# Reciprocal roots of a four-layer kernel: from Newton steps on VectorE to a power instruction on GpSimd

## The reference, cut to what matters

```python
# layer 0: attention, then a second norm whose result is added
ln = (h - mu) / jnp.sqrt(var + EPS) * ln_g + ln_b            # before attention
h1 = out + hidden;  h2 = _sln(h1, ...);  return h2 + h1      # after it, over all tokens
# layer 1: attention with q and k normalised over each head's 64 numbers, then 8 experts
(x - m) * jax.lax.rsqrt(v + EPS) * g + b                     # tokens, heads of q and k, experts
# layer 2: attention and feed-forward, each behind a norm
(x - mu) * jax.lax.rsqrt(var + EPS)
# layer 3: the same with a root mean square in place of the variance
x * jax.lax.rsqrt(jnp.mean(x * x, axis=-1, keepdims=True) + EPS)
```

## Time and profile before

| | us |
|---|---|
| median of 3 runs | 3143.8 |
| lowest, highest | 3141.02, 3148.51 |
| the profiled execution's own time | 3146.93 |
| its span, from first to last instruction | 3145.1 |
| TensorE busy | 2813.3 |
| VectorE busy | 1723.7 |
| ScalarE busy | 916.6 |
| GpSimd busy | 332.6 |

### The profile page before, as it was taken

How to read it: one execution, slowest core, us unless ns; L and a number is a source line. 1 busy time by engine, 2 the same in 40 slices (tenths; PEclk the granted TensorE clock), 3 DMA queues, 4 the chain that set the end, 5 groups by cost and what they waited for, 6 DMA issues and landing times.

```text
span 3145.1 us, 68238 instructions
## 1 busy us (share of the span) xinstructions
PE 2813.3 (89%) x27492; PEld 2032.2 (65%) x27492; DVE 1723.7 (55%) x4229; ACT 916.6 (29%) x1647; POOL 332.6 (11%) x390
## 2 busy tenths in 40 slices
PE   7999699999999933998699999998997989979999
PEld 6788556666666631665588888885443877755555
DVE  5666677777777676231444444443333888842221
ACT  2333255555555500221122222222211233311110
POOL 1111001010010101232011111110000111100000
PEclk9999799999999955999799999998998899989999
DMA  5000000000000031342300000000000000000000
GB/s 184 0 0 0 8 17 27 24 23 27 20 27 20 18 114 50 85 126 47 109 0 0 0 0 0 0 0 1 0 0 0 1 0 0 0 1 14 14 14 14
DMA packets 62313, 77.40 MB, mean 25 GB/s; under 512 B 12640, under 2 KB 52064, under 8 KB 61728
## 3 DMA queue, kind: packets, MB, share of 16 engines
q1 hardware_dynamic: 56096, 67.88, 6.5%
q0 software_dynamic: 6144, 8.52, 1.4%
HBM read 59.33 MB, written 17.06 MB: 24 GB/s over the span
## 4 chain that ended last, share of the span: by engine, by line
PE 54%; DVE 29%; issue 9%; ACT 4%; DVEq 2%; DMA 1%; POOL 0%; SPq 0%; ACTq 0%; POOLq 0%
PE psS L1079 7%; PE psW L293 6%; PE psW L286 5%; DVE work L653 5%; PE psP L463 4%; PE psP L1052 4%; PE psP L1046 4%; PE psS L1073 4%; PE psO L1046 4%; PE psO L1052 3%; DVE work L655 2%; PE psO L408 2%; PE psP L455 2%; PE psO L326 2%; PE psP L392 2%
## 5 line engine op out<-in xcount | busy, mean ns | idle before, releaser
L293 PE MATMUL psW<-r,work 128*128 128x512 f32 (+1 forms) x1280 | 557.0, 567 | 5.5 <-DVE work L690 3.7
L286 PE MATMUL psW<-work,r 128*128 128x128 f32 x3072 | 388.2, 285 | 21.7 <-DVE work L642 16.1
L286 PEld LDWEIGHTS psW<-work,r 128*128 128x128 f32 x3072 | 366.2, 198 | 42.4 <-DVE work L642 31.0
L931 ACT ACTIVATE work<-work 128x512 f32<-128x512 f32 x256 | 161.2, 630 | 628.4 <-DVE work L655 628.4
L293 PEld LDWEIGHTS psW<-r,work 128*128 128x128 f32 x1280 | 225.4, 192 | 173.3 <-issue 156.9
L979 POOL TENSOR_TENSOR work<-work 128x512 f32<-128x512 f32 x128 | 130.7, 1042 | 1274.1 <-DVE work L664 1274.1
L1079 PE MATMUL psS<-r,work 128*128 128x256 f32 x1024 | 225.3, 381 | 6.1 <-DVE work L1149 5.3
L1079 PEld LDWEIGHTS psS<-r,work 128*128 128x128 f32 x1024 | 193.2, 190 | 36.0 <-DVE work L1149 6.1
L392 PE MATMUL psP<-consts,work 128*128 128x128 f32 x1024 | 153.1, 285 | 55.7 <-ACT work L931 50.0
L655 DVE TENSOR_TENSOR work<-psS,work 128x512 f32<-128x512 f32 x256 | 177.0, 692 | 16.3
L653 DVE TENSOR_REDUCE work<-psS 128x8 f32<-128x512 f32 x256 | 174.8, 683 | 11.5 <-PE psS L372 9.7
(11 more groups left out here) (194 smaller groups left out, 4236.9 us busy)
## 6 DMA issues: line engine op xcount, KB each, us to landing
r<-in_l_fc SPq DMA_DIRECT2D x16, 1024.0 KB
work<-mod_rows SPq DMA_DIRECT2D x64, 128.0 KB, 2.9
r<-in_l_w SPq DMA_DIRECT2D x2, 3072.0 KB, 14.6
x<-in_x SPq DMA_DIRECT2D x8, 512.0 KB, 10.0
gather_table<-work SPq DMA_DIRECT2D x32, 128.0 KB, 1.8
moe_sum<-work SPq DMA_DIRECT2D x32, 128.0 KB, 1.7
x<-moe_sum SPq DMA_DIRECT2D x4, 1024.0 KB, 9.4
out<-x SPq DMA_DIRECT2D x8, 512.0 KB, 2.9
```

The costliest lines, as they stand in the source:

```text
L286: ins = nc.tensor.matmul(ps[:, q * P:(q + 1) * P], w[:, k, lo + q * P:lo + (q + 1) * P], L.hT[:, k, :], start=(k == 0), stop=(k == KC - 1))
L293: ins = nc.tensor.matmul(ps[:, 0:width], L.hT[:, k, :], w[:, k, lo:lo + width], start=(k == 0), stop=(k == KC - 1))
L931: nc.scalar.activation(E, E, ACT.Exp, scale=scale).then_inc(L.s[f"exp{i}"].sem, 1)
```

## The change

All 50 roots move to GpSimd. `dve_rsqrt` and its buffer go. A root is now two instructions on GpSimd: an addition of eps, and, after a wait for that addition's semaphore, a power with exponent -0.5. Both take their constant from a column of a small array, broadcast to the shape, which GpSimd fills with three memsets at its start.

For ten of the roots VectorE raises a semaphore (`dve_ask_root`) and waits for another (`dve_take_root`). In layer 0's loop the request is made at the end of steps 4, 12 and 20 and the wait stands at the end of steps 5, 13 and 21; in between GpSimd does the root, behind its bias sum of step 4, 12 and 20, and its program of layer 0 is written out tile by tile instead of run as a loop. In all other places VectorE waits at once.

In layer 1, GpSimd waits for the fourth sum (semaphore r3) and for the variance (new semaphore var), behind the two multiplications of the step. The division by 64 goes: the variance is multiplied by 64 when it is copied, eps is 64 times as large, the root of the variance is multiplied by 8 when it is copied back, and the gains of q and k get a factor 8 in the setup. In the experts, GpSimd's step t first does the root of expert t+1, then the gathers of expert t+2 and the scatters of expert t.

```diff
-        def dve_rsqrt(ch, out, var):
...
+        def dve_ask_root(v, name):
+
+            v.sem_inc(ro["var"], 1)
+
+        def dve_take_root(v, name):
+            v.wait_ge(ro["root"], 2 * (ROOTS.index(name) + 1))
+
+        def root_on_pool(g, out, var, eps, done, count):
+
+            def const(name):
+                at = ROOT_CONSTS.index(name)
+                one = root_consts[:, at:at + 1]
+                return (one.unsqueeze(2) if len(var.shape) == 3 else one).broadcast_to(list(var.shape))
+
+            nc.gpsimd.tensor_tensor(out, var, const(eps), ALU.add).then_inc(done.sem, 1)
+            after(g, done, 2 * count - 1)
+            nc.gpsimd.tensor_tensor(out, out, const("minus_half"), ALU.pow).then_inc(done.sem, 1)
+
+        def pool_root(g, name, out, var):
+            g.wait_ge(ro["var"], ROOTS.index(name) + 1)
+            root_on_pool(g, out, var, "eps", Signal(ro["root"], 0), ROOTS.index(name) + 1)
...
-                    nc.vector.tensor_copy(L.ss33[:, 32:33], mv[:, 0, 1:2])
-            after(v, L.s["r3"], n + 1)
-            ch.link(nc.vector.tensor_scalar(L.ss, L.ss, 1.0 / 64, None, ALU.mult))
-            dve_rsqrt(ch, L.ss33, L.ss33)
+                    nc.vector.tensor_scalar(L.ss33[:, 32:33], mv[:, 0, 1:2], 64.0, None, ALU.mult
+                                            ).then_inc(L.s["var"].sem, 1)
+            after(v, L.s["root"], (n + 1) * 2)
             if norm_too:
-                nc.vector.tensor_copy(rstd[:, bass.ds(n + 2, 1)], L.ss33[:, 32:33])
+                nc.vector.tensor_scalar(rstd[:, bass.ds(n + 2, 1)], L.ss33[:, 32:33], 8.0, None, ALU.mult)
...
+            def head_roots(n, norm_too):
+
+                after(g, L.s["r3"], n + 1)
+                if norm_too:
+                    after(g, L.s["var"], n + 1)
+                root_on_pool(g, L.ss33, L.ss33, "eps64", L.s["root"], n + 1)
...
+                    if L.li == 1 and ahead:
+                        head_roots(t + 1, ahead == 3)
                     return
...
+                if L.li == 0 and t % 8 == 4 and t < NT - 8:
+                    k = t // 8 + 1
+                    pool_root(g, f"l0 {k}", rstd[:, 8 * k:8 * k + 8], moments[:, 8 * k:8 * k + 8, 1])
...
-                    ch.link(ins)
-                    dve_rsqrt(ch, Q.stat[:, :, 2], Q.stat[:, :, 1])
+                    ins.then_inc(Q.s["f_var"].sem, 1)
+                    after(v, Q.s["f_root"], (n + 1) * 2)
...
+            def root(n, u):
+
+                after(g, Q.s["f_var"], n + 1)
+                root_on_pool(g, Q.stat[:, :, 2], Q.stat[:, :, 1], "eps", Q.s["f_root"], n + 1)
+
             def first():
                 gather(0, 0, 0)
                 gather(1, 1, 0)
+                root(0, 0)
 
             def step(t, u, half, ahead):
+                if ahead:
+                    root(t + 1, 1 - u)
                 if ahead == 2:
                     gather(t + 2, u, half + 1)
```

More of the change, by code:

```diff
@@ L221, in build_program @@
         st = sems("st", "out tab gates idx rows")
+        ro = sems("ro", "consts var root")
+        ROOT_CONSTS = ["minus_half", "eps", "eps64"]
+        root_consts = sb("root_consts", [P, 3])
         chain_dve = sem("chain_dve")
@@ L268, in __init__ @@
                     self.s |= signals("rows_in", NT * 32)
+                    self.s |= signals("root", NT * 2)
                 self.loads = {0: 2, 1: 3, 2: 4, 3: 5}[li]
@@ L551, in four @@
             return ap.rearrange("p k (b n) -> p k b n", n=N)
-        def dve_rsqrt(ch, out, var):
[L556 to L573, removed]
+        ROOTS = ["l0 0", "l0 1", "l0 2", "l0 3", "l1 all", "l1 two", "l2", "l2ff", "l3", "l3ff"]
+        def dve_ask_root(v, name):
[13 more added lines that the diff above has]
+            root_on_pool(g, out, var, "eps", Signal(ro["root"], 0), ROOTS.index(name) + 1)
         def dve_moments(ch, t):
@@ L603, in dve_first_block @@
                 dve_group_moments(ch, i)
-            dve_rsqrt(ch, rstd[:, 0:8], moments[:, 0:8, 1])
+            dve_ask_root(v, "l0 0")
+            dve_take_root(v, "l0 0")
         def dve_next_block(v, ch, t):
             k = t // 8 + 1
-            if k == 4 or t % 8 not in (1, 3, 5):
+            if k == 4 or t % 8 not in (1, 3, 4, 5):
+                return
+            if t % 8 == 4:
+                dve_ask_root(v, f"l0 {k}")
                 return
             if t % 8 == 5:
-                dve_rsqrt(ch, rstd[:, 8 * k:8 * k + 8], moments[:, 8 * k:8 * k + 8, 1])
+                dve_take_root(v, f"l0 {k}")
                 return
@@ L779, in first @@
                 if L.li == 1:
-                    dve_rsqrt(ch, L.rstd0, moments[:, :, 1])
+                    dve_ask_root(v, "l1 all")
+                    dve_take_root(v, "l1 all")
                     for n in range(2):
                         dve_second_norm(v, ch, L, n)
-                    dve_rsqrt(ch, rstd[:, 0:2], moments[:, 0:2, 1])
+                    dve_ask_root(v, "l1 two")
+                    dve_take_root(v, "l1 two")
                 elif L.li != 0:
-                    dve_rstd(ch, rms=L.li == 3)
+                    dve_rstd(v, ch, f"l{L.li}", rms=L.li == 3)
                 dve_norm(v, ch, L, 0)
@@ L967, in masks @@
                 ins.then_inc(L.s["mask"].sem, 1)
-            def first():
+            def head_roots(n, norm_too):
[3 more added lines that the diff above has]
+                root_on_pool(g, L.ss33, L.ss33, "eps64", L.s["root"], n + 1)
+            def first():
+                if L.li == 1:
+                    pool_root(g, "l1 all", L.rstd0, moments[:, :, 1])
+                    pool_root(g, "l1 two", rstd[:, 0:2], moments[:, 0:2, 1])
+                    head_roots(0, True)
+                if L.li == 2:
+                    pool_root(g, "l2", rstd[:, :], moments[:, :, 1])
+                if L.li == 3:
+                    pool_root(g, "l3", rstd[:, :], rstd[:, :])
                 if not L.wide:
@@ L986, in step @@
                                         ALU.add).then_inc(L.s["xb"].sem, 1)
+                if L.li == 0 and t % 8 == 4 and t < NT - 8:
+                    k = t // 8 + 1
+                    pool_root(g, f"l0 {k}", rstd[:, 8 * k:8 * k + 8], moments[:, 8 * k:8 * k + 8, 1])
+            if L.li == 0:
+                first()
+                for t in range(NT):
+                    step(t, min(3, NT - 1 - t), t > 0)
+                return
             tiles(g, NT, first, step)
@@ L1020, in __init__ @@
                     self.s |= signals("f_sc", NG * 64)
+                    self.s |= signals("f_var", NG)
+                    self.s |= signals("f_root", 2 * NG)
                     self.s |= signals("f_in0 f_in1 f_ga0 f_ga1", NG // 2 * 64)
@@ L1735, in _ @@
             g.wait_ge(ld["small"], 48)
+            for i, value in enumerate((-0.5, EPS, 64 * EPS)):
+                nc.gpsimd.memset(root_consts[:, i:i + 1], value).then_inc(ro["consts"], 1)
+            g.wait_ge(ro["consts"], 3)
+            pool_root(g, "l0 0", rstd[:, 0:8], moments[:, 0:8, 1])
             g.wait_ge(ld["rows"], 32)
@@ L1744, in _ @@
             pool_attention(g, L[2])
+            pool_root(g, "l2ff", rstd[:, :], moments[:, :, 1])
             following(g, "l2ff")
             pool_attention(g, L[3])
+            pool_root(g, "l3ff", rstd[:, :], rstd[:, :])
 def host_arrays(I):
```

11 lines of the change are left out of this document (6 added, 5 removed), and 2 rows, old and new, of the table W.

## The result

The changed kernel takes 3264.9 us in the median of four runs (3262.9 to 3267.7), against 3146.2 us (3141.0 to 3149.5) for the kernel before on the same chip. The ratio is 1.038, with a 95% interval from 1.036 to 1.040. The forecast was 3126, and the range, which ended at 3243, doesn't hold it. In the profiled executions the span goes from 3145.1 to 3265.9 us, 120.8 more.

A forecast was written before the change was run, and what follows sets the result against it. TensorE was taken to bound the kernel, with Newton almost wholly hidden in layer 1's loop. Gains of 9.5, 6.8 and 4.2 less 2.9 us made 17.6: 3129.3 us profiled, 3126.2 as a median, range 3112 to 3243.

The forecast's parts named there:

- p: Duration of GpSimd's power in each root, estimated at 1.83 us for 33 columns, 1.78 for 32.
- p above 2.9 us: Stated sign of failure: a power on 33 columns longer than this makes TensorE wait in layer 1's loop.
- the capped gain of 4.2 us: Layer 1's loop, 31 roots: the shorter root gains only what TensorE waits there, 4.2 us.
- The high end of p: Power priced as 15 Newton steps done by GpSimd, 5.7 us: 99 us slower, 3243 us in all.
- Rival one: The power is the new wait in layer 1's loop; about 45 us lost at 4.3 us, 3189; chance 0.30.
- Newton was hidden in layer 1's loop: Layer 1: TensorE's products cover the 3.59 us of Newton steps almost wholly; waits total 4.2 us in 27 tiles.
- shorter by more than 0.15 us: Stated sign of failure: layer 1's tiles shortening by more than this, since Newton was held to be hidden there.
- Roots alone: Roots with nothing beside them: five of 32 columns, two short ones and layer 1's first tile gain 9.5 us together.
- Layer 0: Layer 0's loop: three roots of 8 columns, asked for a tile ahead, vanish from the time, a gain of 6.8 us.
- Experts: Expert loop: root queued behind four scatters makes TensorE 0.48 us late in six of eight tiles, a 2.9 us loss.
- Code that has to be fetched at each change of operation: GpSimd fetches the power's code after a multiply or scatter, 1.28 us in each root: 3154 us; chance 0.08.
- Hand-overs of 0.5 us: Hand-overs with GpSimd cost this instead of 0.14 us, each root 1.08 dearer: 3143 us; chance 0.10.

The follow-up runs named there:

- e3: Kernel before, all roots Newton on VectorE, with eleven extra linked VectorE multiplies behind each layer 1 q and k root: 3272.8 us, ratio 1.0390.
- e8: Kernel before, all roots Newton on VectorE, with five extra linked VectorE multiplies behind each layer 1 q and k root: 3202.3 us, ratio 1.0186.
- e1: Changed kernel with only layer 1's q and k roots back to Newton steps on VectorE: 3151.0 us, ratio 1.0009 against the kernel before.
- e11: Kernel before with only GpSimd's loop of layer 0 written out, no root moved: 3148.4 us, ratio 1.0005.
- e4: Changed kernel with thirteen extra GpSimd operations (powers of various shapes and values, an add, a multiply) at the end of layer 2: 3268.7 us.
- e6: Kernel before with layer 1's q and k roots on GpSimd in two parts, all other roots Newton: 3133.5 us, ratio 0.9975.
- e5: Kernel before with layer 1's q and k roots on GpSimd in two parts, plus layer 0's, setup's and the two-column roots: 3136.4 us, ratio 0.9982.

## Why the prediction was wrong

**The step that failed is the size of p.** I took 30 passes of the add's slope, 50 ns a column, "because the power has the add's shape". It is 158 ns a column and 5.66 us for 33. The shape says nothing of what is done to an element. The condition under which the forecast would fail, p above 2.9 us, was exceeded by a factor of two. With p as it is, the new wait in layer 1's loop, 2.65 us in every tile, took the place of the capped gain of 4.2 us. The high end of p, Newton's 15 steps at GpSimd's price, was 5.7 us; that it is exact is luck, since no run shows that the power is made of such steps.

**The high end's time was still too low, because the clock had no term.** At p = 5.7 I had 3243, and 3264.9 came. For layer 1's loop I had 86 us and 110.2 were measured. The waiting itself was if anything over-priced (77.5 us). What is missing are the matmuls behind each wait, at a lower clock: 32.7 us here. e3 shows that a wait alone brings them, and e8 that they go with the clock and not with the wait. Rival one, the power as the new wait, named the right mechanism and place, and undersized it for the same reason: each 0.1 us of p above 2.9 was to cost 3.1 us in the loop, and it cost 110.2 / 27.6 = 4.0 (5.66 - 2.9 being 27.6 such steps).

**Newton was hidden in layer 1's loop**, as I held: with it back (e1) the loss is gone. But "shorter by more than 0.15 us" was named as what would refute me, and without the power the tile is 0.35 us shorter. The cap of 4.2 us, from the earlier trace rows, should have been about 10, since the idle time in a bracket leaves out the overlap that the wait also undoes.

**Roots alone.** Before layer 3 the first modulation comes after the root like this (after; before in the earlier trace rows):

```profile
2539.76 0.24 POOL L572 TENSOR_TENSOR rstd<-rstd,root_consts 128x32 f32<-128x32 f32 x1 [252.37 <-DVEq L560]
2540.08 5.42 POOL L574 TENSOR_TENSOR rstd<-rstd,root_consts 128x32 f32<-128x32 f32 x1
...
2545.53 0.35 DVE L638 TENSOR_SCALAR work<-x,rstd 128x256 f32<-128x256 f32 x1 [5.97 <-POOL rstd L574]
2546.03 0.66 PE L282 MATMUL psW<-consts,work 128*128 128x128 f32 x2 [10.41 <-DVE work L638]
```

TensorE's wait there grew from 7.83 to 10.41 us. I had a gain of 0.9 for each of five. For four of them it is a loss: TensorE's waits at the starts of layer 2, its feed-forward, layer 3 and its feed-forward grew by 2.3, 2.4, 2.6 and 2.5 us. At the start of layer 1, where a short root that got faster stands behind the long one, its wait grew by 0.7. The hand-overs were rightly sized, if a little high: 5.97 - 5.42 - 0.24 leaves 0.31 us for three.

**Layer 0** held: 6.8 us forecast, 7.5 in the three tiles. The root is asked for a tile ahead, so even 1.73 us for 8 columns doesn't show. That GpSimd's written-out loop costs nothing held for the whole run (e11, within 0.1%), if not for each tile: with the Newton root still there, one tile took 13.52 us instead of 11.97.

**Experts.** The wait came where I said: the root is queued behind the four scatters, and VectorE's normalisations wait for it.

```profile
1404.54 1.56 POOL L1293 DMA_INDIRECT moe_sum<-work  x1 [0.30 <-issue]
1405.55 0.79 POOL L572 TENSOR_TENSOR work<-work,root_consts 128x4 f32<-128x4 f32 x1
1406.42 1.04 POOL L574 TENSOR_TENSOR work<-work,root_consts 128x4 f32<-128x4 f32 x1
1407.59 1.76 DVE L1148 TENSOR_SCALAR work<-work 128x256 f32<-128x256 f32 x4 [7.62 <-POOL work L574]
...
1409.40 1.09 PE L1070 MATMUL psW<-consts,work 128*128 128x128 f32 x8 [0.18 <-DVE work L1148]
```

The stage lost 2.2 us (235.0 against 232.8 us from the first scaling L1161 of the transposed tokens to the last L1217; 1124 and 1180 are their lines before), near the 2.9 forecast. The nearness is partly luck. Add and power took 1.83 us, not 0.57. But the add began 1.01 us after the start of the last scatter, where I had taken the 1.97 us to the next gather, and the normalisations were 0.27 us shorter than I had. From the last scatter's start to the transposes are thus 4.86 us, where the forecast has 4.99. TensorE waits 0.18 us here and up to 0.36 in the other four tiles, 1.4 us in all.

**The other rivals.** Code that has to be fetched at each change of operation isn't seen: the power takes 5.65 to 5.66 us in all 32 tiles, where multiplies always come between, and 5.65 to 5.80 us in e4, where it follows another power. Hand-overs of 0.5 us aren't either; they are 0.1. The Trainium skill's GPSIMD Engine Reference, section 3, which speaks for VectorE in elementwise work, pointed the right way, but its factor of about two would have made 2.1 us of my 1.83. This case's trace has 0.16 us a column for the power and 1.7 ns a column for the multiply: the factor between the engines is not the matter, the operation is.

**The sum.** Of the 120.8 us 110.2 are layer 1's loop, 2.1 lie before its first residual sum, and 8.5 behind its last. The 2.1 are made up so: layer 0's loop gives 6.7, but it starts 0.9 later, the stretch from it to layer 1's first modulation is 2.6 longer, and from there to the first residual sum are 5.4 more. Behind the last, the four long roots with 9.8, the experts' 2.2 and some 2.8 for layer 3's round of 10.70 us would make 14.8. The largest part of the difference from 8.5 is at the start of layer 3, and it is the clock again, this time in favour of the change; about 3 us of it are spread over the stages and not traced. From TensorE's first transposes to the first residual sum are 31.0 us (2546.03 to 2577.0) against 34.4 before (2425.57 to 2460.0). The stretches of the two kernels, before and then after, with TensorE's granted clock in the fourth column:

```profile
2434.00:2443.00 9.00, 8.36 (x84) 0.51 0.01 3
2443.00:2452.00 9.00, 8.59 (x144) 0.69 0.01 2
```

```profile
2554.50:2563.50 9.00, 8.32 (x84) 0.50 0.01 2
2563.50:2572.00 8.50, 7.69 (x156) 0.98 0.01 2
```

At the start of a stage, behind a long pause, the clock was at the upper level sooner after than before. The longer wait isn't needed for that: in e6, whose root before layer 3 is Newton's and whose wait is 7.82 us, the same stretch takes 31.0 us too, with a clock of 0.96 where before has 0.69. Nine other profiled executions with a wait of 7.8 us, that of before among them, take 33.7 to 34.5 us; four with waits of 5.2 or 10.4 us take 30.8 to 31.1. So the 3.4 us are not safely the change's own; what decides is open.

## What to carry to other kernels

An operation that no row shows isn't bounded by another of the same shape: give its price the whole span between the ends, and ask first at which price the forecast turns and how much of the span lies on either side. Here it turned at about 2.9 us, half way between 0.24 and 5.7. A wait on TensorE's path costs more than its length: 2.5 us of it cost 3.5 here. And a slow engine can still be the right one where the work is asked for early or cut in parts so that other work covers it: the same power made the kernel 3.8% slower in one piece and, in two parts and only where it was covered, 0.5% faster than before.

## What the runs showed that I had not expected

- GpSimd's power on f32 takes 0.60 us for one column and 158 ns for each further one, up to 5.66 us for 33; 64 or 32 rows cost what 128 do, and values of 0.001, 1.7 and 400 the same.
- Waits of 1.3 us, once in a tile of some 23 us, bring the lower clock behind every second of them (0.96 over the loop in e8), and there it costs 1.5 us a tile. With waits of 2.65 us it is 0.92 in e3 and 0.93 in the change.
- A loop that isn't edited can change its length by 0.06 to 0.2 us a round when code ahead of it on the same engine changes, visible as 0.23 to 0.46 us of "issue" before the round's first instruction. In this kernel that is worth up to 6 us for a loop (layers 2 and 3 in e5), a fifth of a percent, and more than some of the terms that I summed.
- The idle time that a timeline shows ahead of a matmul group understates the wait: 0.15 us shown, 0.31 lost.
